# The expert layers over 59 tiles of 512 rows with 11 tiles of 256 rows between them

## The reference

```python
h = tok_ref(x, ...)                                  # patches @ W.T + b, layer norm
h = h + attn_ref(layernorm(h), Wq, bq, Wk, bk, Wv, bv, scale)
f = layernorm(h)
rh = relu(f @ router_w1 + router_b1)
top_w, top_i = top_k(softmax(rh @ router_w2 + router_b2), 2)      # of 6 experts
gates = softmax(top_w)
h1 = relu(f @ w1[e] + b1[e]); h2 = relu(h1 @ w2[e] + b2[e]); y = h2 @ w3[e] + b3[e]   # 256x256 each
h = h + sum over the two chosen experts of gate * y[e]
```

## Time and profile before

| what | value |
| --- | --- |
| median of 3 runs | 1299.24 us (1298.17 to 1303.66) |
| the profiled execution's own time | 1298.97 us |
| its span, first to last instruction | 1297.2 us |
| busy PE, PEld, DVE, ACT, POOL | 94%, 83%, 82%, 65%, 71% |
| products of 128x512 in the second part | L777, 1608 |
| products of 128x256 in the second part | L804, 1608 |
| granted clock, mean | 0.984 |
| bytes moved by the DMA queues | 180.45 MB |

### The profile page before, as it was taken

One profiled execution on the slowest core, in us unless ns is written; L12 is line 12 of the kernel. 1 busy time (PEld: TensorE's weight loads), 2 busy tenths in 40 slices (PEclk: granted clock), 3 DMA queues, 4 the chain that ended last, 5 costly groups with the idle time before them and its releaser, 6 DMA issues. The chain is left out here.

```text
span 1297.2 us, 28243 instructions
## 1 busy us (share of the span) xinstructions
PE 1222.9 (94%) x7888; PEld 1075.9 (83%) x7888; DVE 1060.5 (82%) x3593; ACT 843.3 (65%) x1838; POOL 918.8 (71%) x740
## 2 busy tenths in 40 slices
PE   4999999999999999999898999999999999999993
PEld 4888888888888888888677888888888888889883
DVE  5789999999999999998777778777777777878783
ACT  2677677667667757776655667676666666666662
POOL 2127777877777777787788777777676767767776
PEclk8899999999999999999999999999999999999997
DMA  4224555544444444554469989766696687687745
GB/s 133 83 85 126 146 144 150 138 116 115 120 118 115 126 112 109 156 167 123 118 182 203 255 188 234 134 114 127 112 236 108 125 193 154 108 185 164 128 55 60
DMA packets 137193, 180.45 MB, mean 139 GB/s; under 512 B 38345, under 2 KB 103501, under 8 KB 137037
## 3 DMA queue, kind: packets, MB, share of 16 engines
q0 software_dynamic: 75456, 69.19, 32.9%
q1 hardware_dynamic: 60316, 108.67, 27.5%
q10 hardware_dynamic: 1264, 0.79, 0.2%
HBM read 159.01 MB, written 101.49 MB: 201 GB/s over the span
## 5 line engine op out<-in xcount | busy, mean ns | idle before, releaser
L559 POOL DMA_INDIRECT out<-yo,tail x268 | 434.2, 1620 | 168.8 <-issue 138.1
L510 POOL DMA_INDIRECT expert_rows<-rec,row_i x256 | 354.7, 1386 | 72.6 <-issue 59.4
L979 ACT ACTIVATE h2v<-bank,small 128x512 f32<-128x512 f32 x134 | 92.3, 690 | 204.6 <-PE bank L777 203.3
L804 PE MATMUL bank<-w_sb,h_hi 128*128 128x256 f32 x1072 | 208.8, 288 | 4.1 <-issue 3.6
L777 PE MATMUL bank<-x_hi,w_sb 128*128 128x512 f32 x536 | 178.6, 395 | 5.7 <-DVE x_lo L1337 4.8
L777 PE MATMUL bank<-h_hi,w_sb 128*128 128x512 f32 x536 | 177.4, 392 | 1.4 <-issue 1.4
L804 PEld LDWEIGHTS bank<-w_sb,h_hi 128*128 128x128 f32 x1072 | 171.6, 191 | 4.9 <-issue 4.2
L804 PE MATMUL bank<-w_sb,h_lo 128*128 128x256 f32 x536 | 151.7, 283 | 0.0
L777 PEld LDWEIGHTS bank<-x_hi,w_sb 128*128 128x128 f32 x536 | 101.8, 190 | 27.5 <-issue 5.0
L777 PEld LDWEIGHTS bank<-h_hi,w_sb 128*128 128x128 f32 x536 | 101.0, 188 | 21.4 <-issue 1.7
L985 ACT ACTIVATE yo<-yo,gcol 128x256 f32<-128x256 f32 x268 | 113.9, 498 | 4.7 <-DVE yo L1368 4.7
(11 more groups left out here) (190 smaller groups left out, 3113.3 us busy)
## 6 DMA issues: line engine op xcount, KB each, us to landing
w_sb<-split_weights SPq DMA_DIRECT2D x189, 512.0 KB
xg<-expert_rows SPq DMA_DIRECT2D x67, 530.0 KB, 4.7
out<-h SPq DMA_DIRECT2D x32, 496.0 KB
split_weights<-half_w SPq DMA_DIRECT2D x36, 256.0 KB, 4.1
small<-in_esmall SPq DMA_DIRECT2D x67, 134.0 KB
x_in<-in_x SPq DMA_DIRECT2D x32, 250.0 KB, 10.7
expert_rows<-pad_rows SPq DMA_DIRECT2D x9, 530.0 KB, 9.1
raw_w<-in_eweights SPq DMA_DIRECT2D x36, 128.0 KB, 4.1
```

Source lines behind the costliest of these rows:

```text
L510: pool.indirect_dma_start(rows_dram, bass.IndirectOffsetOnAxis(ap=row_i[0:TOK, slot, j, k:k + 1], axis=0), rec[0:TOK, slot, j, :], None).t ...
L559: pool.indirect_dma_start(out, bass.IndirectOffsetOnAxis(ap=tail[:, t % TAILS, j, E8:].bitcast(I32), axis=0), yo[:, t % YO, j, :], None, c ...
L804: mm = pe.matmul(banks[6 + b][:, (j % 2) * D:(j % 2 + 1) * D], act[:, c, j * P:(j + 1) * P], w[:, 2, c, wh, :], start=(c == 0 and p == 0), ...
L979: act.activation(h2v[:, m, :], banks[bank + m][:], ACT.Relu, bias=small[:, t % SLOTS, DC + m:DC + m + 1]).then_inc(S["h2_v"], 1)
```

## The change

The second part gets a second kind of tile. `ORDER` is the list of pieces: 59 tiles of 512 rows, and 11 halves of 256 rows after tiles 10, 15, 20, ..., 55 and 58. Each piece has a place q in the order, by which all semaphores of PE, ACT and DVE are counted now. An expert has floor((n + 255) / 512) big tiles, up to 59 in all, and what is left goes to halves of its own. With these inputs the big tiles of experts 0 to 5 are 3, 6, 16, 18, 11 and 5; expert 2 has one half, expert 5 has eight, and two halves are spare.

Halves have buffers of their own, one of each: rows, tail, small values, outputs, gates and one set of weights, whose three loads are made for each half without a condition. Spare rows written in the first part fall from five pieces to three. The core of the diff:

```diff
-NT = (NTOK * TOPK + NE * (TILE - 1)) // TILE
+NT = (-(-NTOK * TOPK // HALF) - NE) // 2
+NH = (NTOK * TOPK + NE * (HALF - 1)) // HALF - 2 * NT
+FIRST_HALF, HALF_STEP = 10, 5
+AFTER = [min(FIRST_HALF + HALF_STEP * k, NT - 1) for k in range(NH)]
...
+            def half_layers(k, layers):
+                expert = half_table_of(k, HEXPERT, NE - 1)
+                for n in layers:
+                    if k:
+                        q = HALVES[k - 1].q
+                        wait_apart(sp, (S["h1_ps"], S["h2_ps"], S["y_ps"])[n], (q + 1) * 2, S["sp_passed"])
+                    sp.dma_start(half_sb[:, n, :, :, :]..., split_dram[...]).then_inc(half_w_loaded[n], 16)
+            def half_rows(k):
+                row = half_table_of(k, HROW, NE * REGION + SPARE * TILE - HALF)
+                expert = half_table_of(k, HEXPERT, NE - 1)
+                if k:
+                    ...                                   # txT_ps, tail_kept, y_dve of the half before
+                sp.dma_start(half_xg[:]..., rows_dram[bass.ds(row, HALF), :]...)
+                sp.dma_start(half_small[:], esmall[bass.ds(expert, 1), :, :]...)
+            def half_loads(t):                            # at the end of SP's iteration t
+                if t == FIRST_HALF - HALF_STEP:           # 5
+                    sp.wait_ge(S["halves"], HALVES_AT)
+                    sp.dma_start(half_dram, u_coli[0:NH, :]).then_inc(S["half_tab_kept"], 16)
+                if t == FIRST_HALF - HALF_STEP + 1:
+                    sp.wait_ge(S["half_tab_kept"], 16)
+                    sp.dma_start(half_tab[:], half_dram...).then_inc(S["half_tab_loaded"], 16)
+                if t == FIRST_HALF - HALF_STEP + 2:
+                    sp.wait_ge(S["half_tab_loaded"], 16)
+                for k in range(NH):
+                    since = t - (FIRST_HALF + HALF_STEP * (k - 1))
+                    if since == 2:
+                        half_rows(k)
+                        half_layers(k, (0,))
+                    if since == 3:
+                        half_layers(k, (1, 2))
...
             def add_tile(t):
...
+                if t.n - 1 in AFTER:
+                    pool.wait_ge(S["half_added"], (AFTER.index(t.n - 1) + 1) * HALF_ADDED)
+            def add_half(t):
+                for b in (AFTER[t.n] - 1, AFTER[t.n]):
+                    pool.wait_ge(y_added[b % 2], landed(b))
+                add_rows(t, S["half_added"])
...
             def layer(t, n, bank, hi, lo, read, count, done):
-                w = w_sb[t % WSLOTS]
+                w, cols = weights_in(t), t.blocks * P
...
-                            mm = pe.matmul(banks[bank + m][:], w[...], act[:, c, :],
+                            mm = pe.matmul(banks[bank + m][:, 0:cols], w[...], act[:, c, 0:cols],
...
-            for t in range(2, NT):
+            for t in ORDER[2:]:
...
+                if t.q == 4:
+                    half_table()                          # DVE, 19 small operations
```

More of the change, by code:

```diff
@@ L13 @@
+from collections import namedtuple
 from contextlib import ExitStack
@@ L69 @@
 PADS_AT, TABLE_AT = 1, 20
+HROW, HEXPERT, HCOLS = range(3)
+HALVES_AT = 19
+FIRST_HALF, HALF_STEP = 10, 5
 DRAIN = G + 1
+Piece = namedtuple("Piece", "q half n blocks")
+AFTER = [min(FIRST_HALF + HALF_STEP * k, NT - 1) for k in range(NH)]
+assert len(set(AFTER)) == NH and AFTER[-2] + 3 < NT
+ORDER = []
+for big in range(NT):
+    ORDER.append(Piece(len(ORDER), False, big, TB))
+    if big in AFTER:
+        ORDER.append(Piece(len(ORDER), True, AFTER.index(big), HB))
+BIG = [t for t in ORDER if not t.half]
+HALVES = [t for t in ORDER if t.half]
 assert (DECIDE + 1) * GT * TOPK > NE * (EARLY * TILE - 1)
@@ L271, in landed, with gated_up_to, rows_in, kept_tail @@
             return (t // 2 + 1) * ADDED if t >= 0 else 0
+        def gated_up_to(q):
+            return sum(t.blocks for t in ORDER[:max(q, 0)])
+        def rows_in(t):
+            return half_xg[:] if t.half else xg[:, t.n % SLOTS, :, :]
+        def kept_tail(t):
+            return half_tail[:] if t.half else tail[:, t.n % TAILS, :, :]
+        def small_in(t):
+            return half_small[:] if t.half else small[:, t.n % SLOTS, :]
+        def sums_out(t):
+            return half_yo[:] if t.half else yo[:, t.n % YO, :, :]
+        def gate_out(t):
+            return half_gcol[:] if t.half else gcol[:, t.n % YO, :]
+        def weights_in(t):
+            return half_sb if t.half else w_sb[t.n % WSLOTS]
+        def rows_here(eng, t):
+            if t.half:
+                eng.wait_ge(S["half_rows_loaded"], 16 * (t.n + 1))
+            else:
+                eng.wait_ge(rows_loaded[t.n % SLOTS], t.n // SLOTS * 16 + 16)
+        def small_here(eng, t):
+            if t.half:
+                eng.wait_ge(S["half_small_loaded"], 16 * (t.n + 1))
+            else:
+                eng.wait_ge(small_loaded[t.n % SLOTS], t.n // SLOTS * 16 + 16)
+        def layer_here(eng, t, n):
+            if t.half:
+                eng.wait_ge(half_w_loaded[n], 16 * (t.n + 1))
+            else:
+                eng.wait_ge(w_loaded[t.n % WSLOTS][n], fetched(t.n))
+        def added_before(eng, t, ring):
+            if t.half:
+                wait(eng, S["half_added"], t.n * HALF_ADDED)
+            else:
+                wait(eng, y_added[t.n % 2], landed(t.n - ring))
         def sent_to(slot, groups):
@@ L988, in _ @@
             pipeline(step)
-            second_values(1, 4)
-            gate_rows(0)
-            for t in range(2, NT):
-                first_values(t, 0 if t == 2 else 2)
-                if t + 1 < NT:
-                    read_rows(t + 1, 2 if t == 2 else 0)
+            second_values(ORDER[1], 4)
+            gate_rows(ORDER[0])
+            for t in ORDER[2:]:
+                first_values(t, 0 if t.q == 2 else 2)
+                if t.q + 1 < len(ORDER):
+                    read_rows(ORDER[t.q + 1], 2 if t.q == 2 else 0)
@@ L1339, in rows_low @@
             def rows_low(t):
[L1340 to L1343 removed]
+                cols = t.blocks * P
+                added_before(v, t, TAILS)
+                v.wait_ge(S["txT_ps"], t.q * 2 + 2)
@@ L1356, in rows_out @@
             def rows_out(t):
-                at = t * 4
-                wait(v, S["y_gated"], (t - 1) * TB)
-                wait(v, y_added[t % 2], landed(t - YO))
-                v.wait_ge(small_loaded[t % SLOTS], t // SLOTS * 16 + 16)
-                v.tensor_tensor(gsel[:], tail[:, t % TAILS, :, 0:E8],
-                                small[:, t % SLOTS, 2 * DC + D:SMALL].unsqueeze(1).to_broadcast([P, TB, E8]),
+                at, each = t.q * 4, t.blocks // 2
+                gates_of = half_gsel[:] if t.half else gsel[:]
```

316 lines of the change are left out of this document (202 added, 114 removed).

## The result

The kernel after the change takes 1306.68 us (median of 20 runs, 1302.68 to 1316.16) against 1298.99 us for the kernel before on the same chip: 1.0063 times as long, interval 1.0050 to 1.0076. The forecast was 1295.2 us and "within 0.5%" the likeliest case; the time lies inside the range of 1284 to 1309 but on the slower side of that bound. The profiled execution took 1306.97 us, its span is 1305.2 us.

The account below looks back on a forecast made before the run. The second part was taken to be bound by what PE issues. From 1298.97 us, -16.8 for PE's work, seams and the end plus 13.0 for SP's late loads gave -3.8: 1295.2 us, range 1284 to 1309.

Parts of the forecast that it names:

- PE's work and the seams: On PE, eight big tiles go and eleven halves come, 20.9 us less issued; seams cost 0.15 us per half, 4.95 in all.
- rival D: On PE, a 256-column product costs three quarters of a long one, 13 us over 11 halves: 1308; chance 0.04.
- SP's work: In SP's queue, a half adds 5.9 us of issues; late loads make PE wait, 13.0 us net in all.
- x: Start of the third layer of tile 57 on PE, forecast as 1260.23 - 15.0 + 13.0 = 1258.2.
- Rival C: In SP's queue, SP falls behind for good at 11.2 us per half: about 1317; chance 0.19.
- DVE's second table: On DVE at tile 4, 19 more operations take 3.8 us; costs PE nothing, at most 2 us.
- POOL in between ... Nothing: In POOL's queue, landing waits around halves fit, 46.7 us per group against PE's 51.0; no cost up to landings of 5 us.
- still owed: On POOL at tile 57, 0.7 us of delay remaining from the half after tile 55.
- The end: POOL's last adds and landings after tile 57's third layer: span ends 35.2 us behind that layer's start, before it was 37.0.
- rival E: In POOL's queue, landings of 6 us make a group 52.7 us against 51.0: about 1308; chance 0.07.
- two signs of being wrong: On PE, forecast wrong if second-part waits fall outside 8 to 20 us in sum, or a half exceeds 5.3 us.
- The sign that failed: In POOL's timeline, two landing waits of about 3 us were to show around each half.

Follow-up runs that it names:

- own_rows: Changed kernel with the halves' adds going to fixed spare rows, so POOL awaits no landing ahead of or behind a half: 1291.93 us, 0.9945 of the kernel before.
- two_tails: Changed kernel with two buffers for `half_tail` instead of one: 1306.96 us, 1.0074 of the kernel before.
- step4: Changed kernel with halves behind every fourth tile from 10 to 50, eight big tiles following the last: 1289.73 us, 0.9938 of the kernel before.
- cond_12_4: Changed kernel with halves after tiles 12, 16, ..., 52, their weights loaded only if the expert differs from the previous half's: 1304.63 us, 1.0045 of the kernel before.

## Why the prediction was wrong, point by point

*PE's work and the seams: right.* A group of five big tiles and a half from one half's turn to the next takes 51.07 us; forecast 5 x 9.22 + 4.95 = 51.05. PE's timeline:

```profile
865.39 0.60 PE L922 MATMUL bank<-ident,half_xg 128*128 128x128 f32 x4
...
871.44 0.28 PE L933 MATMUL bank<-x_hi,half_sb 128*128 128x256 f32 x1
...
916.46 0.60 PE L922 MATMUL bank<-ident,half_xg 128*128 128x128 f32 x4
```

The 12 products of 256 columns in the half's first layer take from 871.44 to 872.88, 1.44 us, 0.120 each. The forecast's rival D, a short product at nearly the long one's price, is out.

*SP's work: the mechanism right, the size somewhat too large.* At tile 10 PE waits 1.43 + 0.80 + 2.81 = 5.0 us where 8.0 stood, at tile 15 2.2 for 3.0, at tile 54 nothing for 1.0, for the last half's rows 2.0 for 1.5. That x is right to 0.1 us although these waits are 4 us fewer is partly chance: behind the waits PE's granted clock fell, to a mean of 0.85 from 760 to 770 us and 0.83 from 820 to 830, which over these 20 us comes to an estimated 3 us (10 x 0.15 + 10 x 0.17). The third row is the stretch behind the wait of 2.81 us: 0.52, nearly the lower of the clock's two levels (1.2 of 2.4 GHz). The forecast had no term for that. Its other figure for a load, the 3.2 us by the Trainium skill, "DMA: Bandwidth & Descriptors", section "Anatomy of one DMA", is stated there for DMAs that GpSimd issues, and these loads are SP's. The waits that should nearly vanish by it came to 5.0 us at tile 10.

```profile
760.00:770.00 10.00, 7.19 (x47) 6.79 (x46) 6.04 (x15) 5.30 (x12) 5.64 (x4) 0.85 0.94 248
820.00:830.00 10.00, 8.91 (x51) 8.37 (x52) 5.54 (x16) 4.85 (x12) 6.18 (x4) 0.83 1.03 249
767.00:770.00 3.00, 3.00 (x17) 3.00 (x16) 0.79 (x2) 0.00 (x0) 1.50 (x1) 0.52 0.60 185
```

Rival C, SP behind for good, is out: from 850 to 1200 us SP waits for DVE and PE 17.1 us in all, which is slack.

```profile
SPq L105 <- DVE tail L1545: 11.7, 7, 2.1
SPq L105 <- PE bank L922: 5.4, 4, 2.1
```

*DVE's second table: right* in its effect, PE has no wait near 705 us but that of the earlier trace rows. The 19 operations take 2.3 us (698.94 to 701.26), not 3.8.

*"POOL in between ... Nothing" is the step that failed*, and with it the 0.7 us "still owed" in *The end*. It priced the landing at 3.0 us and allowed for 5, and said against its rival E that 3.0 and 3.9 are all that show. That is a misreading of its own trace, for the kernel before waits 5.38 us at the start of expert 2 (tile 15, below) and as long at that of expert 0 (741.58). After the change the waits for landings around halves were 3.0 to 3.4 us where the DMA share was 0.5, and 4.3 to 5.6 where it was 0.93 to 0.95. The bound "nothing up to 5 us" came from the average group: 5 x 7.4 + 3.7 + 2 x 5 = 50.7 of 51.1 us. This says only that the lag doesn't grow from group to group. It doesn't say that a lag is given back: with landings of 5 us a group gives back 0.4. So what half 6 and the expert change at tile 43 add, about 5 us each (6.28 us of wait at 1129.98), stays until the end, and the end is what counts. own_rows has nearly the same wait at the same tile, 5.99 us, and a lag of 4.1 behind it; there it is gone by tile 46. First the row that the forecast passed over, from POOL's timeline of the kernel before, then that of own_rows:

```profile
821.05 1.57 POOL L559 DMA_INDIRECT out<-yo,tail  x1 [5.38 <-issue]
```
```profile
1127.24 1.55 POOL L711 DMA_INDIRECT out<-yo,tail  x1 [5.99 <-DMA out<-yo,tail]
```

The timeline names ACT as the releaser at 1129.98; but ACT had gated tile 43 by 1120.5 and only the next tile's rows at that time, and own_rows' row names the landing. Some adds were dearer than 1.85 us apart as well: 1244.06, 1246.05, 1248.12, 1250.16 are 2.03 apart. The DMA share was 0.46 there (1244 to 1252 us), so a full queue isn't the reason; it stays open. Rival E had this mechanism, with a chance of 0.07. That its time, 1308, is so near is partly chance: it took landings of 6 us at all eleven halves, while up to half 5 they are mostly 3 and leave no lag.

The forecast's two signs of being wrong both look at PE and say little here: from 750 us on PE's waits of 0.4 us and more come to 18.9 us (bounds 8 to 20; 23.0 with the two at 703 and 712 us, which the kernel before has too), and a half takes 5.0. The sign that failed is the one on POOL, two landing waits of about 3 us around each half.

*"The end"*: the order of the steps was right (the last add's issue ends at 1301.11 and its landing takes 4.1 us; the landing ahead of the last half 3.06), the start of the chain 12.2 us late.

Shown by a kernel of its own: that the landing waits in POOL's queue cost some 15 us (own_rows), that the single `half_tail` costs nothing while the lag is there (two_tails), that the halves' places alone decide between 1307 and 1290 (step4). Only read beside each other: long landings and a high DMA share. Open: why the lag differs from run to run, and how much of the wait at tile 10 is SP's issues and how much half 0's bytes, since no kernel took away one alone.

## What to carry to other kernels

A wait for a landing in an in-order queue is work of that queue: count it at the longest landing that the trace shows, not at a usual one, and ask how much the queue gives back per piece afterwards, not only whether the average fits. Small pieces with such waits want enough large pieces behind them to pay the lag back: eight were enough in step4, while in cond_12_4 a lag of up to 18.6 us had cost too much before its last six. And the longest new wait of the busiest engine need not be a cause: a kernel that removes just that wait tells.

## What the runs showed of the hardware

POOL's wait for the landing of an indirect add was about 3.0 us in the quietest stretches (a DMA share of 0.5) and 4.3 to 6.8 us in the stretches at 0.92 to 0.95 that are shown; but it was 5.38 us at 0.62 (the kernel before at 821.05) and 3.75 us at 0.95 (the changed kernel at 768.50). The issues of the adds are 1.85 us apart, in some places 2.03, also at a share of 0.46. Behind a wait of 2.81 us PE's granted clock was 0.52 from 767 to 770 us, and behind one of 2.02 us it was 0.58 from 1258 to 1262; behind the wait of 1.43 us at 750.48 it was still 1.00 up to 755. So a wait can cost more than its length, here an estimated 3 us beside the 5.0 and 2.2 us of waits at tiles 10 and 15.
